# GpSimd's gathers: waits for landing between groups of table gathers and between the quarters of the return gathers

## Time and profile before

| | us |
|---|---|
| median of 3 runs | 885.04 (881.66 to 885.18) |
| the profiled execution | 886.06 |
| its span | 884.2 |
| TensorE busy | 691.8 |
| VectorE busy | 566.3 |
| ScalarE busy | 526.3 |
| GpSimd busy | 311.7 |
| mean granted TensorE clock | 0.882 |

### The profile page before, as it was taken

One profiled execution on the slowest core, in us unless ns is written; L12 is line 12 of the kernel. 1 busy time (PEld: TensorE's weight loads), 2 busy tenths in 40 slices (PEclk: granted clock), 3 DMA queues, 4 the chain that ended last, 5 costly groups with the idle time before them and its releaser, 6 DMA issues.

```text
span 884.2 us, 13703 instructions
## 1 busy us (share of the span) xinstructions
PE 691.8 (78%) x5039; PEld 462.4 (52%) x5039; DVE 566.3 (64%) x1081; ACT 526.3 (60%) x1074; POOL 311.7 (35%) x303
## 2 busy tenths in 40 slices
PE   5479849158788897205998899999799999888977
PEld 4268728023345443102555876666478878665632
DVE  5679816257667663002999557886799424666777
ACT  5656613226657563002568448767488658999867
POOL 4666653734756654770000000001898004000000
PEclk8589958569989797556999899999899999999998
DMA  9335722200001001220300000006000000000001
GB/s 312 103 97 159 99 62 66 54 24 24 22 25 29 26 26 35 52 53 14 37 8 1 1 1 1 1 1 241 0 2 1 1 1 1 1 1 1 1 0 48
DMA packets 40273, 36.11 MB, mean 41 GB/s; under 512 B 21800, under 2 KB 30256, under 8 KB 40208
## 3 DMA queue, kind: packets, MB, share of 16 engines
q1 hardware_dynamic: 33616, 21.73, 8.4%
q0 software_dynamic: 6592, 13.51, 6.9%
HBM read 30.11 MB, written 5.11 MB: 40 GB/s over the span
## 4 chain that ended last, share of the span: by engine, by line
PE 55%; another core or an unknown queue 13%; DVE 13%; ACT 13%; issue 3%; DMA 1%; SPq 0%; POOL 0%; ACTq 0%; DVEq 0%; POOLq 0%
PE ps L1340 4%; PE ps L1553 3%; PE ps L1590 3%; PE ps L427 2%; PE ps L2059 2%; PE ps L2323 2%; PE ps L2010 2%; PE ps L996 2%; PE ps L1581 2%; ACT big L2379 2%; PE ps L1571 2%; PE ps L1013 2%; PE ps L212 2%; PE ps L768 2%
## 5 line engine op out<-in xcount | busy, mean ns | idle before, releaser
L1486 POOL DMA_INDIRECT pe<-in_rpe,idx x128 | 125.3, 979 | 44.2 <-issue 34.0
L1949 POOL TENSOR_SCALAR big<-big,wcols 128x256 f32<-128x256 f32 x1 | 0.9, 939 | 207.7 <-DMA big<-in_l3f_w 207.7
L520 ACT ACTIVATE pe<-ps,wcols 128x256 f32<-128x256 f32 x92 | 37.8, 479 | 35.7 <-remote 17.1
L383 POOL DMA_INDIRECT pe<-normed_rows,pe x46 | 48.7, 1058 | 27.8 <-issue 9.4
L1195 ACT ACTIVATE small<-ps 128x512 f32<-128x512 f32 x16 | 9.5, 597 | 75.2 <-remote 62.3
L1256 DVE TENSOR_TENSOR big<-ps,small 128x512 f32<-128x512 f32 x16 | 10.9, 684 | 66.4 <-ACT small L1196 66.4
L427 PE MATMUL ps<-big 128*128 128x256 f16 x276 | 40.3, 299 | 14.6 <-issue 8.5
L1202 ACT ACTIVATE big<-ps 128x1024 f32<-128x1024 f32 x32 | 32.7, 1022 | 26.7 <-PE ps L993 23.1
L1693 ACT ACTIVATE big<-ps,small 128x128 f32<-128x128 f32 x128 | 34.8, 383 | 17.4 <-PE ps L1581 17.4
L1222 DVE TENSOR_REDUCE small<-ps 128x16 f32<-128x1024 f32 x32 | 38.7, 1217 | 9.7 <-PE ps L987 7.1
L1340 PE MATMUL ps<-nT,big 128*128 128x512 f16 x192 | 44.5, 379 | 0.0
(11 more groups left out here) (428 smaller groups left out, 2059.3 us busy)
## 6 DMA issues: line engine op xcount, KB each, us to landing
pe<-in_l2f_w SPq DMA_DIRECT2D x16, 256.0 KB
tile_results<-big SPq DMA_DIRECT2D x23, 128.0 KB
pe<-in_xrow SPq DMA_DIRECT2D x4, 512.0 KB, 3.8
big<-in_l0x_w SPq DMA_DIRECT2D x8, 256.0 KB
pe<-in_rpe,idx POOLq DMA_INDIRECT x128
cT<-in_cT SPq DMA_DIRECT2D x2, 512.0 KB, 5.3
nT<-in_l0x_w SPq DMA_DIRECT2D x4, 256.0 KB
vx<-in_l0x_w SPq DMA_DIRECT2D x4, 256.0 KB
```

The lines of the kernel that those rows point to most:

```text
L383: pool.indirect_dma_start(out=xg16[:, i % RX, h, :, :].rearrange("p r n -> p (r n)"), out_offset=None, in_=xrows_d, in_offset=bass.Indirec ...
L520: ins_ = act.activation(hid32[:, i % RF, f, :], hidden_ps(i, u)[:, f % 2, :], ACT.Relu, bias=wcols[:, bass.ds(at + (COL_AT["l0x_b1"][0] + ...
L1486: pool.indirect_dma_start(out=pe[:, v * D:(v + 1) * D], out_offset=None, in_=ins["rpe"], in_offset=bass.IndirectOffsetOnAxis(ap=idx[:, v:v ...
```

## The change

Four edits, all in GpSimd's program:

- `EARLY` is 16 and `IN_L0` is `EARLY + 12`: two table gathers more ahead of the row gathers, and behind them 12 in place of 16. `IN_L1` becomes 36, so that the steps of attention gather up to v = 80 and 47 are left for the last run.
- In the run behind the row gathers GpSimd waits, at the start of each group but the first, for the landing of the group just before it (`pool_landed`).
- Between the quarters of the return gathers it waits each time for the landing of the quarter just before.
- Before the last run the wait for `A2["pv"]` goes; in the run it waits at the start of each group for the landing of the group just before.

```diff
--- before.py
+++ after.py
@@ -383,12 +383,14 @@
                     pool.indirect_dma_start(out=xg16[:, i % RX, h, :, :].rearrange("p r n -> p (r n)"), out_offset=None, in_=xrows_d,
                                             in_offset=bass.IndirectOffsetOnAxis(ap=gidx[:, g:g + 1], axis=0)).then_inc(s_xg[i % RX], 16)
             for v in range(EARLY, IN_L0):
+                if v > EARLY and v % VG == 0:
+                    pool_landed(pool, v // VG - 1)
                 pool_gather(pool, v)
             for k in range(RY):
                 pool.wait_ge(s_ys[k], 16 * len(range(k, NT, RY)))
             for c in range(NCH):
-                if c == 3:
-                    pool.wait_ge(s_xg[0], returned(0))
+                if c:
+                    pool.wait_ge(s_xg[(c - 1) % 3], returned(c - 1))
                 for b in range(c * BC, (c + 1) * BC):
                     for j in range(PICKS):
                         at = j * B + b
@@ -1180,8 +1182,9 @@
                     pool_queries(pool, b + 2)
                 if b in KEYS_IN:
                     pool_keys(pool, POOL_KEYS[KEYS_IN.index(b)])
-            pool.wait_ge(A2["pv"], B - 2)
             for v in range(IN_L1 + PER_STEP * (B - 1), S):
+                if v % VG == 0:
+                    pool_landed(pool, v // VG - 1)
                 pool_gather(pool, v)
 
         def act_queries(act, c):
@@ -1473,9 +1476,9 @@
             return ap.rearrange("p (f j) -> p f j", j=VG)
 
         QR = 4
-        EARLY = 14
+        EARLY = 16
         PER_STEP = 3
-        IN_L0 = EARLY + 16
+        IN_L0 = EARLY + 12
         IN_L1 = IN_L0 + 8
         qhalf = big[:, 0:QR * NH2 // 2 * S].rearrange("p (r n) -> p r n", r=QR)
 
@@ -1485,6 +1488,9 @@
                 pool.wait_ge(s_pos[g % 2], 16 * VG * (g // 2))
             pool.indirect_dma_start(out=pe[:, v * D:(v + 1) * D], out_offset=None, in_=ins["rpe"],
                                     in_offset=bass.IndirectOffsetOnAxis(ap=idx[:, v:v + 1], axis=0)).then_inc(s_pos[g % 2], 16)
+
+        def pool_landed(pool, g):
+            pool.wait_ge(s_pos[g % 2], 16 * VG * (g // 2 + 1))
 
         def pool_layer4(pool, link):
             pool.wait_ge(M0["w16"], E)
```

## The result

Before: 883.35 us, median of 4 runs (880.94 to 885.18). After: 808.47 us, median of 4 runs (805.86 to 811.31). The ratio is 0.9154, with a 95% interval of 0.9112 to 0.9197. The profiled execution has a span of 806.0 us and a mean clock of 0.932. Later sets of runs, on four chips, are told with the experiments: on two of them the kernel before took 885 and 899 us, on the other two 762 and 763. The kernel after was run on one of these last two, and there it is 0.7% slower than the kernel before.

A forecast was written before the change was run, and what follows sets the result against it. It took late signals and slow dispatch during GpSimd's unbroken gather runs to bound the kernel. Gains of 13.4, 10.9 and 49.3 sum to 73.6 us, from 886.1 to 812.5, or 811 on the median's scale; range 788 to 850.

The forecast's parts named there:

- The theory: GpSimd's unbroken gather runs choke signals and dispatch between engines; a pause of about a microsecond clears it; main case 0.68.
- Rival (c): The holes have another cause, such as code loading, and the waits are beside the point: 883 to 889 us; chance 0.04.
- the second hole: 25.96 us from 157.90 without an engine, during 32 return gathers, said to close 0.5 to 6 us behind the run's end.
- EARLY, cost nothing: Two more table gathers ahead of the row gathers, 2.5 us, fit into GpSimd's 3.71 us of idling and cost nothing.
- Table run behind the row gathers, 13.4: Twelve table gathers for 16, with two waits: at most 17.6 us to gain, less 3.4 and 0.8, gives 13.4.
- Return gathers, 10.9: Four quarters of eight gathers, each after the last has landed: at most 18.8 us to gain, less 7.9, gives 10.9.
- three quarters run beside the chunks: 7.9 us stay: Eight gathers in a row still hurt, by 2.64 us as at 220.46, for three return quarters beside the first layer's feed-forward.
- just hidden: The fourth return quarter lands at 191.1, just before VectorE wants it at 191.4.
- Last run, 49.3: 47 table gathers with 11 waits at attention's end: at most 54.2 us to gain, less 4.9, gives 49.3.
- (a): Rival: relief, but every burst of gathers still costs one late signal of about 2.6 us: 841 us; chance 0.14.
- (b): Rival: the pause is too short, so the choke lasts as long as the now longer run: 911 us, slower; chance 0.10.
- (d): Rival: gathers take 1.96 us each once VectorE works, so the last run lands at 459: 838 us; chance 0.04.

The follow-up runs named there:

- runs 1 to 8: Eight edits of the kernel after, on two chips where the kernel before took 884.87 and 898.56 us; ratios to it 0.9044 to 0.9713.
- runs 5 to 8: Four edits of the kernel after's landing waits, on a chip where the kernel before took 898.56 us; ratios to it 0.9044 to 0.9532.
- c_rests_early: Kernel after with the wait for A2["pv"] kept and last-run landing waits only before gathers 84, 88, 92, 104 and 116; 815.60 us, ratio 0.9044 to the kernel before.
- pause_by_work: Kernel after with three memsets of a scratch tile in place of each landing wait of the last run; 857.83 us, ratio 0.9532 to the kernel before.
- sooner_in_fours: Kernel after with the wait for A2["pv"], more landing waits, four gathers in steps 11 to 14 and EARLY 14; 776.89 us, ratio 1.0217 to the kernel before.

## Why the prediction was right, point by point

**The theory.** Unbroken runs of gathers delay signals and dispatch, and waits for landing clear it: shown on the chips of runs 1 to 8, where taking the waits out of any one of the three places brings that place's hole back. What the gathers choke isn't shown. It takes something besides the program: two other chips don't have it. Every execution on record was also recorded by the profiler, so it isn't shown either that one without its records has the holes. Rival (c), a cause in which the waits play no part, is wrong for the chips that have the holes.

One clause of the theory failed: "a pause of about a microsecond clears it". A rest of 1.16 us in each four gathers left nearly the whole hole (0.9532). The prediction priced the wait at 1.6 us between gathers, and it was 1.75 to 3.30. That the real wait was the longer one was luck; no run tried a pause of just 1.6 us. And one of the readings was wrong: the second hole doesn't close behind its run of gathers. Its piece ends at 157.90 + 25.96 = 183.86, ahead of the end of the last return gather at 185.68.

**EARLY, cost nothing.** It cost 1.33 us. The cover was there, GpSimd still idles 2.82 us before the first row gather, but VectorE's L636, from which that gather's indices come, waited 2.00 us, until 33.22, for a "remote" signal, which came behind the thirteen gathers in a row that ended at 31.4. On the free chip it waited 0.44 us, until 32.00. The step left out what the prediction itself says of runs of gathers.

**Table run behind the row gathers, 13.4.** 13.99 by the first return gather, and 15.3 with the 1.33 put back. The two waits left 2.33 and 2.49 us, not 1.6; six gathers in a row remain at its start (two of rows, four of the table), and the 3.4 us charged for them didn't show in the chain. About 8.5 of it are the waits.

**Return gathers, 10.9.** 17.9, near the bound of 18.8. The failed step is "three quarters run beside the chunks: 7.9 us stay": eight gathers in a row with 1.8 to 2.1 us behind them left no stall in the chain between 131.90 and 184.10. The 2.64 us at 220.46, from which the 7.9 came, has its like in the kernel after: the eight table gathers, which still have no wait, now run from 178.12 to 187.9, and the chain has 3.75 us of "issue" at 185.89 at their end. So the row was read rightly and its eight do stall; those of the returns did not, on this chip. On the chip of runs 5 to 8 they did: `c_rests_early` and `pause_by_work`, with the same waits, have pieces of 3.42 and 2.75 us, and of 3.45, 2.70 and 3.85, in this part. So the term is too large for the chip of the result and about right for the other. The prediction called it its most doubtful one. A second step failed too: the gathers of the fourth quarter are not "just hidden". VectorE waits for the landing of each of the three later quarters before it adds up their rows:

```profile
155.22 2.33 DVE L708 SCALAR_TENSOR_TENSOR pe<-pe,small 128x128 f32<-128x128 f32 x8 [2.11 <-DMA pe<-tile_results,pe]
166.75 2.33 DVE L708 SCALAR_TENSOR_TENSOR pe<-pe,small 128x128 f32<-128x128 f32 x8 [3.91 <-DMA pe<-tile_results,pe]
```

(and 2.46 us at 178.26), and from 131.90 to 166.73 the chain is the issue and landing of the first three quarters' gathers. Nearly all of the gain lies in the first quarter: its sums begin 14.2 us behind the first return gather (146.12 against 131.90), where they began 29.3 us behind it (175.23 against 145.89). That is 15.1 us; the other quarters gave 2.8.

**Last run, 49.3.** 46.7. The residual is 7.5 us for 4.9: what stayed is 8.09, 3.76 and 3.99 us, all before layer 3 begins, the first of it beside nine in a row, which the prediction named without charging for them. Past 324 the chain has no such piece up to layer 3.

**The sum.** 73.6, of which the moments show 13.99 + 17.94 + 46.72 = 78.65 and the medians 885.04 - 808.47 = 76.6. The errors are -7.0 in the returns and -1.9 in the table run, against +1.3 in EARLY and +2.6 in the last run: part of them cancelled, which is luck.

**The signs.** Most came; three did not. The clock did not stay at its higher level through the end of attention: it is 0.76 in 296 to 324. Between the groups lie 1.75 to 3.30 us and not 1.3 to 1.9. And "remote" waits of several microseconds, the sign of (a), are there in the last run: 8.98 us beside the nine in a row, and 3.0 to 3.8 us beside groups of four.

**The rivals.** (a), every burst costs a late signal: not at 2.6 us each, but something of the kind is there. A step of attention with three gathers takes 0.9 us more on a choked chip than on a free one. (b): the hole was nearly whole with a rest of 1.2 us in four gathers, not with the wait's 1.75 to 3.3. (d): true in kind, gathers of 3.94 to 6.62 us in four kernels, but only beside the rows of twelve TENSOR_SCALARs, which the kernel after escaped by 11.6 us (389.0 to 400.6) on its chip and did not escape on the free one.

**The bounds.** "Nothing left of any hole ... 791" took the row gathers' stretch as unharmed but for 6%, and attention's steps as unharmed. The free chips give the kernel before 762, some 30 us below that. Behind layer 3's first matmul the kernel after takes the same time on both kinds of chip, so by an estimate these 30 us are late signals too, spread thinly where the chain shows no piece for them. No trace of the kernel before on a free chip shows it.

## What to carry to other kernels

Where a one-core profile puts time down to "another core or an unknown queue", lay it beside GpSimd's timeline: if a piece begins some gathers into an unbroken run, put a wait for landing behind every four to eight of them. Attention was late sooner than layer 3, so the part with the many small instructions is the one to begin with. Time such a fix on more than one chip before it is kept: here it gains 8.5% on one kind and loses 0.7% on the other. And end a run of GpSimd's gathers before VectorE starts a long row of TENSOR_SCALARs like these twelve, or the gather ends behind them.

## What the runs showed of the hardware that I had not expected

- The same program on the same inputs: 880.9 to 887.3 us and 892.0 to 903.1 on some chips, 758.4 to 764.7 on two others. The traces differ in late signals between engines while GpSimd issues gathers; what makes the difference isn't known.
- A wait for landing left 1.71 to 4.56 us between issues, and 6.06 once (in `sooner_in_fours`); two gathers in flight at 1.4 us, or a rest of 1.2 us in four, relieved little (0.964 and 0.953 against 0.971 with no rest).
- The length of run that is borne depends on the other engines' work: 28 gathers beside the first 41 us of layer 3 in one kernel, seven of a run of twelve beside layer 3 in another, fewer than nine at the end of attention.
- A gather issued while VectorE runs twelve TENSOR_SCALARs of 128x512 f32 (6.21 us), or up to 0.3 us before they begin, ends 0.11 to 0.13 us behind them: eight times in eight, in five runs. Four gathers issued 0.8 to 1.2 us before they begin took 0.94 to 1.41 us, and those beside four TENSOR_SCALARs of 128x128 f32 (1.1 us) 0.94 to 1.05.
